# One level of Strassen's algorithm for the attention scores, and attention in steps of 512 keys with a running maximum

## The reference

```python
def _gat_layer(x, W, adj):
    proj = x @ W
    Wh, Ws = jnp.split(proj, 2, axis=-1)
    scores = Wh @ Ws.T
    a = jax.nn.softmax(scores, axis=-1) * adj
    out = a @ Wh
    out = out + x
    return jax.nn.leaky_relu(out, NEG_SLOPE)
...
x = _layernorm(x + _L0_gnn_ref(x, adj, L0_gnn_W_stack), axis=-1)
x = _layernorm(x + _L1_gnn_ref(x, adj, L1_gnn_weight), axis=-1)
```

## Time and profile before

| | |
|---|---|
| median of 3 runs | 2333.96 us |
| the profiled execution | 2334.25 us |
| its span, first to last instruction | 2332.3 us |
| PE, DVE, ACT, POOL busy | 95%, 47%, 24%, 19% |
| mean granted clock of PE, as a share of full | 0.983 |
| matmuls | 10532 |
| scores, L599: x4368, busy | 893.4 us |
| mix, L614: x4056, busy | 883.7 us |
| second graph layer, L923: x676, busy | 149.4 us |
| projection, L384 and L395, busy | 141.9 and 137.1 us |
| DMA engines, mean busy share of q1 | 52.4% |

### The profile page before, as it was taken

How to read it: one execution, slowest core, us unless ns; L and a number is a source line. 1 busy time by engine, 2 the same in 40 slices (tenths; PEclk the granted TensorE clock), 3 DMA queues, 4 the chain that set the end, 5 groups by cost and what they waited for, 6 DMA issues and landing times. The chain is left out here.

```text
span 2332.3 us, 29117 instructions
## 1 busy us (share of the span) xinstructions
PE 2217.7 (95%) x10532; PEld 1037.2 (44%) x10532; DVE 1089.7 (47%) x2243; ACT 562.4 (24%) x881; POOL 439.2 (19%) x241
## 2 busy tenths in 40 slices
PE   3998999999999999997997999999999999998699
PEld 1443444444444444443444444444444444443244
DVE  2434665565556556654433434434444443443254
ACT  5332222122212221222332222222122122121000
POOL 0001222122212212220001331232232232131000
PEclk9999999999999999998998999999999999999799
DMA  7425654564465446534425776766866866874775
GB/s 235 93 62 142 145 120 106 135 144 105 111 144 138 99 122 144 128 94 114 93 61 143 157 157 160 178 148 152 185 143 151 189 147 148 182 158 105 245 248 181
DMA packets 557830, 333.24 MB, mean 143 GB/s; under 512 B 487056, under 2 KB 493840, under 8 KB 556944
## 3 DMA queue, kind: packets, MB, share of 16 engines
q1 hardware_dynamic: 549040, 296.76, 52.4%
q0 software_dynamic: 1248, 22.15, 5.2%
q10 hardware_dynamic: 7488, 13.63, 1.8%
HBM read 211.48 MB, written 46.01 MB: 110 GB/s over the span
## 5 line engine op out<-in xcount | busy, mean ns | idle before, releaser
L599 PE MATMUL p_scores_a<-keys_t,q_t_a 128*128 128x512 f16 (+1 forms) x4368 | 893.4, 366 | 23.0 <-DVE row_a L712 13.2
L614 PE MATMUL p_out_a<-values,probs_t_a 128*128 128x512 f16 x4056 | 883.7, 379 | 0.0
L692 POOL TENSOR_TENSOR kept_probs_a<-row_a,adj_row_a 128x896 f32<-128x896 f32 x208 | 424.6, 2055 | 1615.2 <-ACT row_a L659 1520.7
L599 PEld LDWEIGHTS p_scores_a<-keys_t,q_t_a 128*128 128x128 f16 x4368 | 429.2, 98 | 489.3 <-DVE row_a L712 14.1
L614 PEld LDWEIGHTS p_out_a<-values,probs_t_a 128*128 128x128 f16 x4056 | 396.9, 98 | 467.9
L659 ACT ACTIVATE row_a<-row_a,shift_a,scales 128x896 f32<-128x896 f32 x208 | 222.5, 1071 | 994.7 <-DVE shift_a L722 994.7
L712 DVE TENSOR_SCALAR_CACHE_REDUCE row_a<-p_scores_a 128x512 f32<-128x512 f32 (+1 forms) x364 | 237.1, 653 | 479.3 <-PE p_scores_a L599 472.6
L727 DVE SCALAR_TENSOR_TENSOR row_a<-kept_probs_a,row_a 128x896 f16<-128x896 f32 x208 | 239.6, 1152 | 281.0 <-ACT row_a L674 276.7
L674 ACT ACTIVATE row_a<-kept_probs_a 128x896 f16<-128x896 f32 x208 | 186.1, 895 | 229.4 <-POOL kept_probs_a L692 229.4
L923 PE MATMUL p_out_b<-products_b,adj_b 128*128 128x512 f16 x676 | 149.4, 385 | 24.1 <-issue 24.1
L384 PE MATMUL p_values_p<-w_p,x_t_p 128*128 128x512 f16 x624 | 141.9, 388 | 30.9 <-DMA x_t_p<-x_p 30.9
(11 more groups left out here) (83 smaller groups left out, 599.1 us busy)
## 6 DMA issues: line engine op xcount, KB each, us to landing
adj_row_a<-adj_rows SPq DMA_DIRECT2D x104, 448.0 KB, 4.8
adj_row_a<-adj_rows SPq DMA_DIRECT2D x104, 384.0 KB, 4.3
adj_t<-adj_blocks POOLq DMA_DIRECT2D x26, 832.0 KB, 8.8
adj_b<-adj_t SPq DMA_DIRECT2D x26, 832.0 KB, 4.5
x_rows_a<-x_rows SPq DMA_DIRECT2D x52, 256.0 KB, 3.0
rows_p<-x_rows SPq DMA_DIRECT2D x13, 512.0 KB, 5.2
x_rows_p<-x_rows SPq DMA_DIRECT2D x26, 256.0 KB, 3.2
x_mid<-y_rows_a SPq DMA_DIRECT2D x26, 256.0 KB, 2.4
```

Source lines behind the costliest of these rows:

```text
L599: last = pe.matmul(p_scores[:, bank, 0:widths[k]], q_t[:, b, qh, c, :], keys_t[:, kh, c, k * BANK:k * BANK + widths[k]], start=(n == 0), s ...
L614: last = pe.matmul(p_out[:, b], piece[:, ph * blocks[part] + j, :], values[:, vh, k, :], start=(k == 0 and n == 0), stop=(k == T - 1 and n ...
L692: pool.tensor_tensor(kept_probs[:, part % 2, 0:blocks[part] * P], row[:, b, cols], adj_row[:, cols], ALU.mult).then_inc(masked, 1)
```

## The change

**Scores.** The two row tiles 2i and 2i+1 are taken together as a 2 by 2 block matrix: two row tiles by two halves of the 512 features. The keys are taken the same way, in pairs of key tiles. Instead of eight block products there are seven (Strassen's algorithm in Winograd's form), on sums of blocks: S1 to S4 of the queries and T1 to T4 of the keys. One step covers 512 keys, that is 256 columns per product and so matmuls of 256 columns. The last 256 keys are done plainly, against `keys_last`. Products that are used twice are copied out by ACT between two of their accumulations (`copy_scores`); the others are added by DVE with the maximum taken in the same instruction (`read_sum`).

**Projection.** `make_rows` makes keys and values as rows, 512 columns of either per matmul. ACT copies them to SBUF scaled (`copy_rows`), POOL forms the eight differences of a pair (`sum_keys`, `sum_queries`), ACT and DVE split blocks and sums (`halve_rows`), SP transposes the seven key blocks, 14 blocks of 128 columns in either half (`turn_keys`), and stores the query sums to DRAM (`store_sums`). Weights are loaded at the start of each `project`. Scales are now per row, and the maximum of the weights takes the place of the column norms that TensorE made.

**Attention.** The unit is a window: one step of one pair, 7 steps per pair (6 of 512 keys, one of 256), 13 pairs, 91 windows a layer. Each window has its maximum; the sum and the accumulated output are multiplied by exp(old shift - new shift). The mix of window w-2 is interleaved with the products of window w; its result is accumulated in SBUF (`accumulate`). The output rows of pair i-1 are made in steps 2 to 4 of pair i (`add_rows`, `make_y`). All loops are unrolled. The adjacency check takes one instruction for two.

```diff
+            keys_t = s.enter_context(nc.sbuf_tensor("keys_t", [P, 2, 7, 2, 2 * WIDE * P], F16))
+            keys_last = s.enter_context(nc.sbuf_tensor("keys_last", [P, 2, DC, 2 * P], F16))
...
+        key_rows = sb("key_rows", [P, 2, 7 * H], F16)
+        sum_rows = sb("sum_rows", [P, 2, 4 * H], F16)
...
+                for i in range(J):
+                    turn_x(2 * i)
+                    turn_x(2 * i + 1)
+                    if layer > 0 and i + RING < J:
+                        load_x(i + RING)
+                    if i >= 2:
+                        turn_keys(i - 2)
+                        store_sums(i - 2)
...
+                def halve_rows(i):
+                    act.wait_ge(x_lo, first_tile + 2 * i + 2)
+                    act.wait_ge(rows_copied, 4 * (first_pair + i + 1))
+                    act.activation(values[:, 2 * i:2 * i + 2, HI], vb[:, A11:S1].rearrange("p (t b) n -> p t (b n)", t=2),
+                                   ACT.Copy).then_inc(values_hi, 1)
+                    used = 4 if i == J - 1 else 7
+                    if i < J - 1:
+                        act.wait_ge(keys_summed, 4 * (first_pair + i + 1 - layer))
+                    if i >= 1:
+                        act.wait_ge(keys_turned[HI], 16 * (layer * (J + 1) + i))
+                        act.wait_ge(keys_lo, first_pair + i)
+                    act.activation(key_rows[:, HI, 0:used * H], ...
...
+                for i in range(J):
+                    for two in (0, 1):
+                        for side in (0, 1):
+                            copy_rows(2 * i + two, side)
+                        if 2 * i + X_RING + two < T:
+                            halve_x(2 * i + X_RING + two)
+                    halve_rows(i)
...
+                def turn_queries(i):
...
+                    for n, (rows, into) in enumerate((
+                            (values[:, 2 * i].rearrange("p h d -> p (h d)"), q_t[:, b, 0:8]),
+                            (s_rows[i * P:(i + 1) * P, :], q_t[:, b, 16:32]),
+                            (values[:, 2 * i + 1].rearrange("p h d -> p (h d)"), q_t[:, b, 8:16]))):
+                        sp.dma_start_transpose(into, rows).then_inc(q_ready[b][n], 16)
...
+                for w in range(windows + 6):
+                    i, step = pair_of(w), step_of(w)
+                    if 0 <= w - 1 < windows:
+                        turn_probs(w - 1, 0)
+                        if w < windows:
+                            load_adj(w, 1)
+                        turn_probs(w - 1, 1)
+                        if w + 1 < windows:
+                            load_adj(w + 1, 0)
...
+                    if step == 2 and i + 1 < J:
+                        turn_queries(i + 1)
+                    if step == 5 and i < J:
+                        load_x(i)
+                    if i >= 1:
+                        if last_layer:
+                            if step == 2:
+                                load_first(i - 1)
+                            if step == 3:
+                                store(2 * i - 2)
+                                turn_bits(2 * i - 2)
+                            if step == 4:
+                                store(2 * i - 1)
+                                turn_bits(2 * i - 1)
+                                store_products(2 * i - 2)
...
+                        else:
+                            if step == 2:
+                                store(2 * i - 2)
+                            if step == 3:
+                                store(2 * i - 1)
...
+                def strassen(w, name, q_block, k_block, first):
+                    cols = slice(step_of(w) * 2 * P, (step_of(w) + 1) * 2 * P)
+                    for c in range(2):
+                        for n, (qh, kh) in enumerate(passes):
+                            last = pe.matmul(bank(w, name), queries(pair_of(w), q_block, qh, c),
+                                             keys_t[:, kh, k_block, c, cols], ...
...
+                    if last_layer and i >= 1 and step in (4, 5):
+                        sign_product(2 * (i - 1) + step - 4, w)
...
+                        strassen(w, SET_A, A11, B11 - 1, True)
+                        free(w, 1)
+                        strassen(w, SET_B, A12, B21 - 1, True)
...
+                    mix(w - 2, 0, 0)
...
+                        pe.wait_ge(scores_read, reads_before(w) + 2)
+                        strassen(w, SET_E, S4, B22 - 1, False)
...
+                def make_y(i, u):
+                    t = 2 * i + u
+                    g = layer * T + t
+                    dve.wait_ge(x_used, used(i, u + 1))
+                    if t >= 1:
+                        dve.wait_ge(stored, 16 * g)
...
+                        dve.wait_ge(row_loaded[u], 16 * (layer * J + 2 * i + 2))
+                        dve.tensor_tensor(work[:, u], y_rows[:], x_rows[:, u], ALU.add).then_inc(x_used, 1)
...
+                for w in range(windows + 6):
+                    i, step = pair_of(w), step_of(w)
+                    if 0 <= w - 1 < windows:
+                        read_rest(w - 1)
+                        make_shift(w - 1)
+                    if w < windows and wide(w):
+                        read_first(w)
+                    if not last_layer and 0 <= w - 1 < windows:
+                        check_adj(w - 1, 0)
+                        check_adj(w - 1, 1)
...
+                    if i >= 1:
+                        if step == 2:
+                            add_rows(i - 1)
+                        if step in ((3, 4) if last_layer else (2, 3)):
+                            make_y(i - 1, step - (3 if last_layer else 2))
+                    if 0 <= w - 1 < windows:
+                        split(w - 1, 0)
+                    if 0 <= w - 2 < windows:
+                        add_total(w - 2)
+                        accumulate(w - 2, 0)
+                    if 0 <= w - 1 < windows:
+                        split(w - 1, 1)
+                    if w < windows and wide(w):
+                        read_second(w)
+                    if 0 <= w - 2 < windows:
+                        accumulate(w - 2, 1)
```

1157 lines of the change are left out of this document (635 added, 522 removed).

## The result

The changed kernel took 2786.62 us in the median of 4 runs (2781.11 to 2788.39), the kernel before 2334.45 us beside it: 1.193 times the time, 95% interval 1.191 to 1.195. The forecast was 2590 us with a range of 2440 to 2720. The direction was right; the time lies 67 us above the range.

The account below looks back on a forecast made before the run. TensorE, 95% busy, was taken as the bound: columns plus edges. Saving 101 us of matmuls against added chain, in-order waits, casts, clock, projection and edges summed to +256 us on 2334, so 2590 us, range 2440 to 2720.

Parts of the forecast that it names:

- first layer, in-order wait: First layer's attention: VectorE waits for the store of row y, queued behind query transposes; 4.8 us per pair, +58 us.
- second layer, in-order waits: Second layer's attention: x lands late behind query transposes, bits' transpose queues behind probability transposes; 11.85 us per pair, +142 us.
- casts: Second layer's attention: GpSimd's casting DMAs share the engines and delay transfers; bounds 0 to +45, taken as +20 us.
- projections: Both projections: a loop between single buffers takes 11.25 us per pair against 10.36, plus x loads in layer two; +38 us.
- matmuls and chain through a step: Attention: fewer matmul columns save 101 us; the chain of engines doesn't fit the 7.2 us step, once per pair, +22 us.
- edges, start and last stage: Outside steady stages: attention starts and first waits +10, layer change and last steps +20, end +14, start +1 us.
- The three pauses per pair: Second layer's timeline: TensorE pauses once inside the third step for x_rows and twice before the sign product for bits_t.
- a loop of 8.0: One attention step: engines chained from a product's read to its last use take 8.0 us, fitting 9.7 but not 7.2.
- The clock: Attention: TensorE runs at a lower granted clock after each of 48 new gaps; 0 to +62, taken as +32 us.
- rival (D): Second layer's attention: low clock holds through steps 3 to 5, 29 us per pair at 1.2 GHz; 2790 us; chance 0.10.
- (B): Attention: the in-order waits mostly aren't there; 2338 us, up to 2400 with a quarter of them left; chance 0.10.
- (C): Whole kernel: faster, score matmuls bound everything and the projection loop has slack too; 2300 us; chance 0.04.

Follow-up runs that it names:

- the last version: Changed kernel with reordered sync list in attention and projections, casts cut and spread over both layers, and the products' store between the probability transposes: 2394 us, ratio to before 1.026.
- the reordered one: Changed kernel with three sync-list moves: second layer's x loads ahead of query transposes, its bits and stores to the step's head, first layer's stores likewise: 2556 us.
- the run: Kernel before with one of GpSimd's 26 casts made and that tile's rows read 26 times: 2338 us against 2334, ratio 1.0019.
- the best version: Same kernel as the last version, with the products' store moved on top of the 2433 us kernel: 2394 us.
- the idle work: Changed kernel plus unused matmuls where TensorE waits in the second layer, 16 of 512 columns before the bits and 30 of 256 in step 3: 2779 us.

## Why the forecast was wrong

The edits of the last version (order in the attention, order in the projections, cut casts, products) take the kernel from 2787 to 2394 us in one chain, so each term of the sum has a measured size. The sizes depend on the order of removal: 25 casts are 97 us in the changed kernel and 113 in the reordered one, where cutting them gives 88 and leaves 23. The row of matmuls and chain is what remains when all others are taken off.

| term | forecast | measured |
|---|---|---|
| first layer, in-order wait, with 8 of the clock | +66 | +58 |
| second layer, in-order waits, with 24 of the clock | +166 | +172 |
| casts | +20 | +111: 88 by cutting, 23 left |
| store of the products, a wait that moving the bits made | none | +39 |
| projections | +38 | +67: 35 by order, 32 left |
| matmuls and chain through a step | -79 | -38 |
| edges, start and last stage | +45 | +43 |

The forecast is 197 us short, by this table: casts 91, in-order waits of the second layer with the products 45, matmuls and chain 41, projections 29, less 10 by which the first layer's waits and the edges came out smaller.

**In-order waits: right** in place and kind. The three pauses per pair stand where the prediction put them. In the first layer undoing them gives the term back within 8 us. In the second it gives 172 for 166, which is partly luck: the moves also made the wait for the store of the products, so with its 39 the order is worth 211, 45 above the term. Part of the pauses was the casts', too: in the pair shown, 4 us of what delays x.

**Casts: the step that failed.** "26 casts, about 15 of them in steps 2 to 5, at 0 to 3 us each" went wrong twice. The row that I had, 5.74 us instead of 1.53 for one transpose, was read as a delay that mostly finds cover, as in the kernel before, where the run shows its cost to be nil. There the unit of work is a row tile with 33.7 us of matmuls. In the change a step is 9.7 us of TensorE around a loop of 8.0, so a delay of 4 us doesn't fit, in any step. All 26 count, at 3.9 us, not 15 at half price. The prediction had the two numbers and never set the 4.2 us of the row against the 1.7 us of slack. It also looked at the wrong side of the row: the price is in when a transpose beside a cast lands (7.0 us after its issue in the changed kernel, 3.2 otherwise, medians), more than in how long it holds SP.

**The store of the products: not a term of the changed kernel.** SP issues it last in steps 4 and 5. In the changed kernel ScalarE never waits for it, since the sign product comes later there; once the bits are turned early, ScalarE waits 50 us in all for it ahead of its next score copies (ACT row above). It is the same kind of wait as the others, one that stood behind them.

**Matmuls and chain: right in sign, too large.** Without the in-order waits the first attention takes 867 us, 19 less than before, where the terms gave 39.5. Its window has 840.7 us of busy time for 13 pairs, 64.7 each instead of 63.5, and the waits that are left come to 26 us, 2.0 per pair instead of 0.85.

**Projection.** 12.5 and 13.4 us a pair, in the stated 11 to 13 or just above; the term was 29 short. The order within SP's list was half of it.

**The clock: its size stays between bounds, rival (D) is wrong, though its 2790 us is the time that came.** After the two long pauses of the pair above TensorE does run at half rate: 9 matmuls of 256 columns take 2.13 us, against 24 in 2.78 before them.

```profile
2054.41 2.78 PE L735 MATMUL p_scores_a<-keys_t,q_t_a 128*128 128x256 f16 x24
...
2083.26 2.13 PE L735 MATMUL p_scores_a<-keys_t,q_t_a 128*128 128x256 f16 x9
```

The granted clock is 0.50 from 2081.6 to 2086.0, which is 1.2 GHz, and 1.00 again, 2.4 GHz, from 2087.8 on. After the pause of 1.91 us it stays at 1.00, and the six matmuls of 512 columns there take 1.45 us as before. But (D) needed 350 us of slow running and 200 us of net loss. TensorE's busy time in the second attention is 74 us above the best version's for the same 5712 matmuls, and the idle work that took 44 of them away won 8. The oscillation that the Trainium skill describes ("TensorE: Matmul & The Clock Gate", HAM oscillation) is there, with a mean granted clock of 0.89 over the stage; the slow running is about a fifth of what (D) made of it (74 of 350 us). That (D)'s figure met the time is luck: casts, the order, matmuls and projections added what the clock didn't.

**(B) and (C) are out**: the waits are there, and with most of them removed the kernel still takes 1.026 times the time of before. 32 us of projection, 25 at the entries, 15 at the layer change and 10 at the end outweigh the 15 won in attention and 8 at the start and in the last stage. Why the projections stay at 154 us wasn't tried further.

## What to carry to other kernels

When a change shortens the unit of work that hides the transfers, every transfer beside it must be priced anew against the slack of the new unit (here 1.7 us), also those that the change doesn't touch and that cost nothing before. Cut such transfers so that each piece fits in the slack, and spread the pieces; cut without spreading was worse than whole. Walk one steady unit through every in-order list, the stores' waiters too: waits that lie in series give back less one at a time (42 and 80 us) than together (172), and a move can bring out the next wait in line (here 39 us).

## What the runs showed that I had not expected

- A DRAM-to-DRAM cast of 832 KB costs 3.9 to 4.5 us each in the kernels whose transposes must land within a step, nothing in the kernel before, where they have a row tile's time, and four quarters of it back to back cost 46 us more over 26 casts than one whole.
- A transpose issued while a cast is under way lands late (7.0 to 7.7 us after its issue instead of 3.2 in the kernels with whole casts, 8.0 instead of 4.8 in the kernel before, medians). An SP instruction behind a cast is often held as well, a transpose 5.21 us instead of 1.24, an adjacency load 2.56 instead of 0.57, but TensorE's wait for the probabilities is for the landing.
- Moving one DMA forward made a wait that wasn't there: ScalarE's 50 us for the store of the products.
- The spread query transposes made the kernel slower by 14 us, though each holds SP for less at a time, and only in the second layer; the cause is open.
